# Attention with the first half of its output projection done inside the units: one more place in each unit from head 8 on

## The reference

```
q, k, v = xn @ q_w.T + q_b, xn @ k_w.T + k_b, xn @ v_w.T + v_b     # 16 heads of 16 columns
attn    = softmax(q k^T / sqrt(16)) v                              # each head, 4096 x 4096 scores
ffn     = bfloat16(fp8(xn) @ fp8(w).T * scales + bias)             # 256 x 256
out     = x + (attn @ out_w.T + out_b) + ffn
```

## Time and profile before

| | us |
|---|---|
| median of three runs | 1885.83 (1885.39 to 1886.12) |
| the profiled execution | 1886.19 |
| its span | 1884.4 |
| ScalarE busy in the span | 1764.0 (94%) |
| TensorE matmul busy | 1647.7 (87%) |
| VectorE busy | 1561.3 (83%) |
| start, until the first exponential | 109.8 |
| attention, until the last exponential ends | 1731 |
| from there to the end of the span | 43.6 |

### The profile page before, as it was taken

The page is one execution under the profiler, slowest core; times in us unless marked ns, Lnnn a source line. Parts: engine busy times, 40 slices in busy tenths (PEclk is TensorE's granted clock), DMA queues, the critical chain, the costliest instruction groups (busy, mean ns, idle before and its releaser), DMA issues.

```text
span 1884.4 us, 74586 instructions
## 1 busy us (share of the span) xinstructions
PE 1647.7 (87%) x33418; PEld 556.7 (30%) x33418; DVE 1561.3 (83%) x1924; ACT 1764.0 (94%) x1944; POOL 23.0 (1%) x41
## 2 busy tenths in 40 slices
PE   7988888888888888888888888888888888888888
PEld 4632222222222222222222222222222222222226
DVE  8687878978787888878787987878888887878788
ACT  2389999999999999999999999999999999999990
POOL 0000000000000000000000000000000000000000
PEclk9999999999999999999999999999999999999999
DMA  6430100000010000000010000001000000001003
GB/s 195 159 91 10 32 10 21 14 18 24 18 24 10 24 12 16 24 18 24 10 31 8 17 20 18 24 10 31 10 23 12 18 24 18 24 10 26 13 14 107
DMA packets 94965, 57.19 MB, mean 30 GB/s; under 512 B 55280, under 2 KB 87280, under 8 KB 94640
## 3 DMA queue, kind: packets, MB, share of 16 engines
q1 hardware_dynamic: 94160, 52.18, 10.3%
q10 hardware_dynamic: 480, 0.20, 0.0%
HBM read 30.54 MB, written 17.30 MB: 25 GB/s over the span
## 4 chain that ended last, share of the span: by engine, by line
ACT 52%; issue 33%; PE 12%; DVE 3%; ACTq 1%; DMA 0%; SPq 0%; DVEq 0%
ACT probs L667 52%; PE banks L1300 3%; PE banks L1259 3%; PE banks L1156 3%; PE banks L1388 1%; PE banks L1167 1%; ACTq L666 1%; DVE o_junk L951 1%; DVE o_sb L950 1%; PE banks L1378 0%; DVE xn_all L821 0%; DMA qk_bias<-in_L_attn_k_b_dram 0%; PE banks L1140 0%; DVE stats L736 0%; DVE x8T L834 0%
## 5 line engine op out<-in xcount | busy, mean ns | idle before, releaser
L667 ACT ACTIVATE probs<-banks 128x1024 f32<-128x1024 f32 x1888 | 1730.9, 1192 | 0.1
L1300 PE MATMUL banks<-probs,v_st 64*32 64x512 f32 x15104 | 1003.8, 590 | 2.2
L1259 PE MATMUL banks<-q_st,k_st 50*32 50x512 f16 x16384 | 792.4, 381 | 212.2 <-ACT probs L667 209.2
L1259 PEld LDWEIGHTS banks<-q_st,k_st 50*32 50x32 f16 x16384 | 232.6, 89 | 1145.5 <-ACT probs L667 1088.9
L984 DVE SCALAR_TENSOR_TENSOR horner<-horner,bits 128x1024 f32<-128x1024 f32 x320 | 393.0, 1228 | 11.0
L1300 PEld LDWEIGHTS banks<-probs,v_st 64*32 64x32 f32 x15104 | 272.0, 106 | 66.8 <-DVE o_junk L951 11.5
L971 DVE TENSOR_SCALAR bits<-banks 128x1024 int32<-128x1024 f32 x160 | 196.0, 1225 | 76.5 <-PE banks L1259 76.3
L984 DVE SCALAR_TENSOR_TENSOR horner<-bits 128x1024 f32<-128x1024 f32 x160 | 196.1, 1226 | 5.5
L989 DVE SCALAR_TENSOR_TENSOR d_probs<-horner,powers 128x1024 f32<-128x1024 f32 x160 | 196.0, 1225 | 5.5
L950 DVE COPY o_sb<-banks 128x512 f32<-128x512 f32 x32 | 22.2, 692 | 130.9 <-PE banks L1300 97.9
L980 DVE TENSOR_SCALAR bits<-bits 128x1024 int32<-128x1024 int32 x160 | 111.1, 694 | 5.5
(11 more groups left out here) (103 smaller groups left out, 428.1 us busy)
## 6 DMA issues: line engine op xcount, KB each, us to landing
k_st<-k_parts SPq DMA_DIRECT2D x102, 64.0 KB, 2.2
q_st<-q_parts SPq DMA_DIRECT2D x198, 32.0 KB, 1.9
k_st<-k_parts SPq DMA_DIRECT2D x102, 60.0 KB, 2.2
q_st<-neg_row SPq DMA_DIRECT2D x264, 1.0 KB, 1.7
xnT_copy<-probs SPq DMA_DIRECT2D x8, 512.0 KB, 3.1
q_parts<-x8T SPq DMA_DIRECT2D x16, 256.0 KB, 3.0
k_parts<-x8T SPq DMA_DIRECT2D x16, 256.0 KB, 2.4
w_f<-xnT_copy SPq DMA_DIRECT2D x16, 256.0 KB, 2.9
```

Of the source, the lines that this page charges most:

```text
L667: act.activation(probs[:, at:at + WIDE * CHUNK].rearrange("p (t c) -> p t c", t=WIDE), banks[:, bank:bank + WIDE, :], ACT.Exp, bias=EXP_SHIFT,
L1259: last = pe.matmul(banks[cols, bank + g, :], k_st[rows, keys], blocks[rows, j], start=True, stop=True, tile_position=(g * GROUP, t * VCOLS))
L1300: last = pe.matmul(banks[VCOLS * qb:VCOLS * (qb + 1), 6 + half, cols], v_st[keys, kt, :], src[keys, g * CHUNK:(g + 1) * CHUNK][:, cols], s ...
```

## The change

`OUT_AT` = 63 puts one more place, `()`, into each unit of the first pass, 66 in all; the pairs behind it move by one. From head 8 on (`FROM_HEAD`), when heads 0 to 7 are complete in `ctxT[:, 0]`, TensorE computes at this place two tiles (256 rows) of the projection's first half: 16 fp32 matmuls of 64 rows by 32 columns of the array and 256 columns, the two halves of the contraction into the two banks of the place's buffer. VectorE adds both banks to the two tiles of `x_all`, one after the other, and frees the buffer; this stands in its program behind the fifth block, before the quantising. In heads 0 to 7 TensorE does nothing at the place and VectorE only counts it as taken. Counts of scores no longer equal counts of places, so waits on `st_done` go through `scores_given`. In the output stage of the first pass only `k = 1` is left. `o_out` becomes eight buffers in `probs`, four groups deep. The second pass, if it runs, loads x anew, adds the bias and computes both halves.

```diff
+    OUT_AT = 63
+    OUT_BUFS = 4
-        o_out = [qt[0], qt[1]]
+        o_out = [probs[:, i * CHUNK:(i + 1) * CHUNK] for i in range(2 * OUT_BUFS)]
-        out_saved = [sem(f"out_saved{i}") for i in range(2)]
+        out_saved = [sem(f"out_saved{i}") for i in range(2 * OUT_BUFS)]
-                for p in range(PAIRS + (not full)):
+                for p in range(PAIRS + 2 * (not full)):
                     if p == MAX_AT and not full:
                         order.append(None)
+                    elif p == OUT_AT and not full:
+                        order.append(())
+        FROM_HEAD = HEADS // KD
+        def scores_given(c, h, n):
+            u, p = divmod(n, c.places)
+            return h * c.head_scores + (u * (c.head_scores // UNITS) + sum(1 for pair in c.order[:p] if pair != ()))
+        def part_tiles(h, u):
+            return 2 * ((h - FROM_HEAD) * UNITS + u)
...
+                for t in range(0, NT, 8):
+                    load_x(t, t + 8, x_back)
                 attend(second)
...
-                    act.wait_ge(c.st_done, h * c.head_places + (n + 1))
+                    act.wait_ge(c.st_done, scores_given(c, h, n + 1))
...
+                def output_part(h, u):
+                    n = u * c.places + OUT_AT
+                    if h < FROM_HEAD:
+                        dve.sem_inc(c.d_taken, 1)
+                        dve.wait_ge(c.d_taken, taken_at(h, u, OUT_AT))
+                        return
+                    bank, t0 = take_bank(h, n), part_tiles(h, u)
+                    rows = x_all[:, t0:t0 + 2, :].rearrange("p t d -> p (t d)")
+                    dve.wait_ge(part_done, t0 // 2 + 1)
+                    dve.tensor_tensor(rows, banks[:, bank, :], rows, ALU.add).then_inc(part_added, 1)
+                    dve.wait_ge(part_added, t0 // 2 + 1)
+                    dve.tensor_tensor(rows, banks[:, bank + 1, :], rows, ALU.add).then_inc(c.d_taken, 1)
+                    dve.wait_ge(c.d_taken, taken_at(h, u, OUT_AT))
...
                             d_block(h, u, n)
                             if n == 0:
                                 sampled_maxima(h, u, lk)
+                        output_part(h, u)
                         if u:
                             quantise_part(h)
...
-                        dve.wait_ge(out_saved[b], n * 16 + OUT_0)
-                        dve.tensor_tensor(o_out[b][:, :], banks[:, 2 + b, :], res[b][:, :], ALU.add
+                        dve.wait_ge(out_saved[n % OUT_BUFS * 2 + b], n // OUT_BUFS * 16 + OUT_0)
+                        dve.tensor_tensor(o_out[n % OUT_BUFS * 2 + b], banks[:, 2 + b, :], res[b][:, :], ALU.add
...
+                def output_part(h, n):
+                    if h < FROM_HEAD:
+                        return
+                    u, bank, t0 = n // c.places, WIDE * ((h * c.head_places + n) % BUFS), part_tiles(h, n // c.places)
+                    buffer_free(h, n)
+                    pe.wait_ge(ctx_saved[t0 // CT % UNITS], SAVES * FROM_HEAD)
+                    for j in range(2):
+                        g, i = divmod(t0 + j, CT)
+                        t = g // UNITS * CT + i
+                        for half in range(2):
+                            rows = slice(half * GROUP, (half + 1) * GROUP)
+                            for q in range(P // VCOLS):
+                                cols = slice(q * VCOLS, (q + 1) * VCOLS)
+                                last = pe.matmul(banks[cols, bank + half, j * D:(j + 1) * D],
+                                                 ctxT[rows, 0, g % UNITS, t, cols], w_sb["o"][rows, 0, :],
+                                                 start=True, stop=True, tile_position=(half * GROUP, q * VCOLS))
+                    last.then_inc(part_done, 1)
...
+                            elif c.order[n % c.places] == ():
+                                output_part(h, n)
...
-                            for k in range(KD):
+                            for k in range(KD) if again else (KD - 1,):
```

More of the change, by code:

```diff
@@ L221, in program @@
         ctx_saved = [sem(f"ctx_saved{i}") for i in range(UNITS)]
+        part_done = sem("part_done")
+        part_added = sem("part_added")
+        x_back = sem("x_back")
+        x_again = sem("x_again")
         ffn_done = sem("ffn_done")
@@ L285, in __init__ @@
                 self.head_takes = UNITS * len(self.takes)
+                self.head_scores = sum(1 for _ in range(UNITS) for pair in order if pair != ())
                 self.from_half_1 = min(p for p, pair in enumerate(order) if pair and pair[0] >= KT // 2)
@@ L384, in _ @@
                          (y_done, 2), (res_done, 2), (out_ready, 2),
-                         (out_saved[0], OUT_0), (out_saved[1], OUT_0)):
+                         *((saved, OUT_0) for saved in out_saved)):
                 sp.sem_inc(s, n)
@@ L513, in attend @@
                         load_rows(c, 1, h * 2 + 2)
-                    sp.wait_ge(c.st_done, h * c.head_places + c.places)
+                    sp.wait_ge(c.st_done, scores_given(c, h, c.places))
                     load_q(sp, c, nxt, 0)
-                    sp.wait_ge(c.st_done, h * c.head_places + (c.places + c.first_read + 1))
+                    sp.wait_ge(c.st_done, scores_given(c, h, c.places + c.first_read + 1))
                     load_k(c, nxt, 2)
@@ L520, in attend @@
                         load_rows(c, 0, h * 2 + 3)
-                    sp.wait_ge(c.st_done, h * c.head_places + (c.places + c.half_0_read + 1))
+                    sp.wait_ge(c.st_done, scores_given(c, h, c.places + c.half_0_read + 1))
                     load_k(c, nxt, 0)
-                    sp.wait_ge(c.st_done, h * c.head_places + c.head_places)
+                    sp.wait_ge(c.st_done, scores_given(c, h, c.head_places))
                     load_k(c, nxt, 1)
@@ L542, in outputs @@
                         sp.dma_start(out_v[:, g * CT + 2 * b:g * CT + 2 * b + 2, :],
-                                     o_out[b][:, :].rearrange("p (t d) -> p t d", t=2)).then_inc(out_saved[b], 16)
+                                     o_out[n % OUT_BUFS * 2 + b].rearrange("p (t d) -> p t d", t=2)
+                                     ).then_inc(out_saved[n % OUT_BUFS * 2 + b], 16)
                 return ok
             def outputs_landed(times):
-                for b in range(2):
-                    sp.wait_ge(out_saved[b], OUT_0 + 16 * times * GROUPS_OUT)
+                for saved in out_saved:
+                    sp.wait_ge(saved, OUT_0 + 16 * times * (GROUPS_OUT // OUT_BUFS))
             attend(first)
@@ L925, in sampled_maxima @@
                     n = u * c.places + MAX_AT
-                    dve.wait_ge(c.st_done, h * c.head_places + (n + 1))
+                    dve.wait_ge(c.st_done, scores_given(c, h, n + 1))
                     turned_maxima(dve.transpose(o_junk[:, :], banks[:, take_bank(h, n), :]), c.d_taken,
@@ L969, in d_block @@
                         dve.wait_ge(c.d_chain, steps)
-                    dve.wait_ge(c.st_done, h * c.head_places + (at + 1))
+                    dve.wait_ge(c.st_done, scores_given(c, h, at + 1))
                     dve.tensor_scalar(words.rearrange("p (t c) -> p t c", t=WIDE), banks[:, bank:bank + WIDE, :],
@@ L1111, in _ @@
             with dve.If(ok < P):
-                for b in range(2):
-                    dve.wait_ge(out_saved[b], OUT_0 + 16 * GROUPS_OUT)
+                for saved in out_saved:
+                    dve.wait_ge(saved, OUT_0 + 16 * (GROUPS_OUT // OUT_BUFS))
+                dve.wait_ge(x_back, 16 * (NT // 8))
+                for t in range(0, NT, 2):
+                    two = x_all[:, t:t + 2, :]
+                    dve.tensor_tensor(two, two, bo_sb[:, :, :], ALU.add).then_inc(x_again, 1)
+                dve.wait_ge(x_again, NT // 2)
                 attend(second)
@@ L1389, in outputs @@
                                                  ctxT[:, k, u, t, :], w_sb["o"][:, k, :],
-                                                 start=(k == 0), stop=(k == KD - 1))
+                                                 start=(k == 0 or not again), stop=(k == KD - 1))
                         last.then_inc(proj_done, 1)
```

## The result

The changed kernel took **1892.41 us** (median of 9 runs, 1890.93 to 1893.89) beside 1886.03 for the kernel before (9 runs, 1885.39 to 1887.58): a ratio of 1.0030, with 95% from 1.0022 to 1.0039. It is slower by 0.3%, more than the 0.2% that this measurement can tell from no change. A ratio is estimated from all runs in the usual, fast state and not from the medians, whose quotient can differ in the fourth place (here 1.0034), and two slow runs stand outside the ratios, one of e5 (2297 us) and one of the kernel before beside e5 to e8 (4064 us).

A forecast was written before the change was run, and what follows sets the result against it. ScalarE's exponentials, 0.917 us each, bound attention; boundaries +4.2, last unit +1.9 and output stage -3.04 summed to +3.05 us on 1886.19, giving 1889.2, with a median of 1888.9. Range 1884.3 to 1893.0, the forecast's own 1887.7 to 1890.5.

The forecast's parts named there:

- The place: Place 63 left empty in heads 0 to 7, 16 units: price 0, up to 1.6 us in all kept for the range.
- The part on TensorE: The 16 fp32 matmuls at place 63, heads 8 to 15: 0.86 us, the same as a weighted sum.
- rival 2: The part costs TensorE over 0.86 us through its weight loads, 1.6 us per extra 0.1: 1889.6 or more; chance 0.19.
- rival 3: The part's weight loads don't overlap matmuls at all, 1.1 us more than taken: +17.6, 1906.5 us; chance 0.03.
- The chain at the boundary: Two adds delay score 0' and three sums follow; exponentials lose 0.28 us at 15 boundaries: +4.2 us, bounds +3.0 to +5.7.
- rival 1: Unit boundaries absorb the wait for the buffer and nothing is late: 1884.7 us (1884.0 to 1886.6); chance 0.22.
- about 0.5 us behind score 65: Sign to look for at the unit boundary: when the second add would release score 0'.
- The second unit's late quantising and take-over: In a head's second unit they move behind the adds; the next unit's exponentials stay on time: price 0, 0.5 in hand.
- The last unit: After the last unit's adds, quantising ends at 1843.99 and the take-over starts at 1844.05, against 1842.16 before: +1.9 us.
- The output stage: Half the projection gone, VectorE's six passes of 3.72 us a group set the pace: 31.0 us, -3.04.
- From the profile to the median: Step from the profiled execution to the median of the runs, taken as 0.36 us below: 1889.2 to 1888.9.
- Rival 4: Faster by over 0.2%, needing no boundary loss and 2.7 us more than rival 1 from the end; chance 0.06.

The follow-up runs named there:

- e5: Changed kernel with a unit's last three weighted sums one place later, behind places 1, 2 and 3 of the next unit: 1886.55 us, ratio 0.9999.
- e8: Changed kernel with unread bf16 matmuls behind each group's projection in the output stage, 24 in the first, 8 in each other: 1891.16 us, ratio 1.0025.
- e3: Changed kernel with place 63 empty in all heads, so the projection's first half is missing from the output: 1884.30 us, ratio 0.9989.
- e1: Changed kernel without VectorE's second add, so the second bank never reaches the output; TensorE's part unchanged: 1885.17 us, ratio 0.9996.
- e12: Changed kernel with TensorE's waits for the next unit's loads made at place 60, not just ahead of score 0': 1889.78 us, ratio 1.0019.
- e4: Changed kernel with a third add in the chain, the second bank being added twice: 1903.14 us, ratio 1.0088.
- e9: The changed kernel itself run once more, as a control: 1891.31 us, ratio 1.0026 to the kernel before.
- e10: Changed kernel with e8's unread matmuls and twelve more between ffn and projection of the second group: 1891.55 us, ratio 1.0027.
- e6: e5 plus the last unit's adds moved behind the quantising and VectorE's flag load behind the last group: 1883.96 us, ratio 0.9986.
- e7: The kernel before with the eight output buffers alone, no place 63 and both halves in the output stage: 1886.34 us, ratio 1.0000.
- e2: Changed kernel with the part as one full-array product a tile into one bank, and one add: 1890.39 us, ratio 1.0019.
- e11: e6 with e10's unread matmuls added: 1883.26 us, ratio 0.9983.

## Why the prediction was right in its steps and short in its sum

The forecast was 1888.9 with an own range to 1890.5, and the time was 1892.4: above the own range, within the range to 1893.0, and slower by over 0.2%, which had a chance of 0.36 against 0.57 for no change. (The sum on record, 4.2 + 1.9 - 3.04, is 3.06 and not 3.05, which changes nothing.) Point by point:

- **The place** (0): right. e3 shows it for all 32 units.
- **The part on TensorE** (0.86 us): right, 1788.52 to 1789.38, its 32 records in the 1.05 that was named. Rival 2 and rival 3 are refuted, and with them the Trainium skill's sentence on LDWEIGHTS and row groups ("TensorE: Matmul & The Clock Gate", Part 3, The mechanism) for this tile shape; that section itself also lets a load run ahead into the background weight buffer, which would allow what the rows show. That the time fell into rival 2's stretch is a coincidence of size: e1 leaves all of the part in and loses nothing at a boundary. And that it lies within the stated range at all, above 1890.5, is owed to this rival's bound of 1893.0, so it is luck.
- **The chain at the boundary** (15 x 0.28 = 4.2): the mechanism was right, link by link, down to the places that are late; rival 1 is refuted. **The failed step is the size of one term**, the 0.06 us from the second add's end to score 0'. It was taken from a weighted sum that waits for VectorE (1790.16 + 0.69 to 1790.92); the measured one was 0.146. VectorE's start behind the part took 0.13, not 0.12. Together they bring score 0' 2.74 us behind the part's start and not 2.64, and this tenth makes 0.369 of 0.28: 1.3 us in the sum. e12 undoes it: with the wait in the weight load the signal takes 0.055 and the loss is 0.278. The bounds of 0.20 to 0.38 held 0.37, because the range had been drawn for a slower signal; the middle was set by the row of another kind of wait. One of the signs was also misstated: "about 0.5 us behind score 65" is the delay of score 0', while the chain's own times put it 0.68 behind score 65 (1785.94 - 1785.26); measured were 0.80.
- **The second unit's late quantising and take-over** (0, with 0.5 in hand): right, no place from 4' on is late.
- **The last unit** (+1.9): the take-over moved by 1.81, from 1.34 to 3.15 behind the last exponential. Another 0.17 came between it and the first output pass. The traces place it between two small passes on `o_zero` and `all_ok` just ahead of the stage, which start 0.39 apart (1853.33, 1853.72) and not 0.22 (1845.93, 1846.15); e1 to e4 don't have it, and its cause is open.
- **The output stage** (-3.04): 3.72 a group, as forecast, and VectorE's six passes are what is late next, but the stage came to 31.5 and not 31.0. The flag's gap, carried over as 1.16 from the kernel before, was 1.44 (VectorE's load of it took 0.84 instead of 0.54 us): +0.3. Two groups at the lower clock: +0.1 each, 0.26 in all by e9 and e10 (a single profile each). The clock was no step of the prediction at all; it had been full through the stage before.
- **The end** (0): +0.2 behind the last pass in this pair of profiles. Over the other kernels it lies between 3.98 and 4.34, with no pattern that a run here explains.
- **From the profile to the median**: the forecast put the median 0.36 below the profiled execution, as three runs of the kernel before had it (nine runs make it 0.16). The changed kernel's median stood 1.0 above its profiled execution in the first set and 0.2 below it in the second, a piece as large as the terms above. The clock goes with it: in the first set five of nine runs had a mean granted clock of 0.995 and took 1892.41 us or more, and the four at 0.996 or 0.997, the profiled one among them, took 1891.68 or less; in e9 the two at 0.995 took 1892.93 and 1893.20, the others 1891.55 or less. So the median depends on how many executions had the lower clock for longer. Where they lost the time isn't profiled, and e10's runs, all at 0.998 or 0.999, still spread from 1890.61 to 1892.30, so the clock isn't shown to be all of it.
- **Rival 4**, a faster kernel by hiding the last unit's quantising, was not what this change does; e6 shows that the idle time for it was there, and that it brought the take-over 1.05 us forward and the first output pass 0.88.

## What to carry to other kernels

Where a dense engine is fed through a small reserve, a new wait is to be judged with the queue behind it: the same 0.39 us cost 0.37 a boundary in front of three long steps and nothing with those three moved one place back (e5). Take a signal's price from a row with the same instruction around the wait, since the price of an instruction that waits for two events isn't that of one that waits for one. And a wait for a buffer that shows 1.3 us may lie on top of another engine's work and be worth nothing (e7), so sum each engine's group first.

## What the runs showed of the hardware that I had not expected

- A semaphore wait on TensorE was a separate instruction when other waits stood before it, and then the signal from VectorE to the first matmul took 0.146 us; folded into the weight load it took 0.055 (changed kernel, e12).
- Full-array products between work in 64x32 and 50x32 tiles took 0.31 us more than the 0.86 us that the products take by themselves (e2).
- With the projection halved, TensorE's clock fell to the 1.2 GHz level for 3.4 or 6.8 us in the output stage of every profile but those of e10 and e11, which fill TensorE's two first gaps; the kernel before and e7 kept 2.4 GHz through it. It fell at the end of a 1.19 us wait (changed kernel, 1857.29) or inside the 2.9 us wait ahead of it (e9, 1854.47); the same 1.19 us wait in the kernel before had no drop behind it. Where no matmuls were added, the second group took from 0.1 us (changed kernel) to 0.6 us (e5) more, and VectorE set the pace of the others.
- VectorE's load of one value into a register left VectorE without a pass for 1.3 us; behind the last group it cost nothing (e6: 29.96 of 30.00 us busy).
